# Causal mask moved from a TensorE product into a fused VectorE add-and-minimum, in a small language-model layer on one core

## The chip, the cores and the metric

The kernel runs on one core of one Trainium2 chip. Such a core has a matrix engine (TensorE, PE in the rows, with its weight loads apart as PEld), a vector engine (VectorE, DVE), a scalar engine (ScalarE, ACT), GpSimd (POOL) and SyncE (SP, which issues transfers). Each takes its own instructions in order, and they meet by semaphores. TensorE writes its results into PSUM, a memory of eight banks of 512 float32 per partition; VectorE and ScalarE read them there. The metric is the device time of one execution in microseconds (us), lower is better.

## The reference

2 x 1024 tokens run through an embedding (hot rows directly, cold rows through a projection), one attention block and one mixture of experts with 16 experts, two of them per token. The change lies in the attention, 16 heads of 32 columns, of which this is the core:

```python
att = jnp.einsum('bhqd,bhkd->bhqk', q, k) / math.sqrt(HEAD_DIM)
causal = jnp.triu(jnp.ones((s, s), dtype=bool), k=1)
att = jnp.where(causal[None, None, :, :], jnp.float32(-1000000000.0), att)
att = jax.nn.softmax(att, axis=-1)
out = jnp.einsum('bhqk,bhkd->bhqd', att, v)
```

## The kernel before, in words

The program runs embedding and first normalisation (to about 135 us of the profile), attention (to about 632 us), then output projection, router, shared expert and routed experts.

Attention is cut into 8 units: 4 groups of 4 heads, times 2 sequences. Unit 0 and unit 7 are written out, units 1 to 6 are three turns of a hardware loop. A unit has 32 steps; step n treats query block i = n // 4 (128 queries) and head h = n % 4, against the (i + 1) x 128 keys up to the diagonal. So a score row has 128 columns at i = 0 and 1024 at i = 7.

What one step asks of the engines:

- **scores** (TensorE, L499): one or two products give the negated scores in one of two pairs of PSUM banks (step n uses pair n % 2); the query side was scaled by -1/sqrt(32) before. They wait until the exponentials of step n - 2 have freed that pair. Then **L501**, a 128 x 128 bf16 product of an identity with `mask_bf`, adds 1e9 above the diagonal to the block of columns that lies on the diagonal. Its end tells VectorE that the scores are ready.
- **row_max** (VectorE, L635): a minimum over the (negated) score row, `nmax`.
- **exp** (ScalarE, L594): exp(nmax - x) for the whole row into `probs`, with the row's sum read out by a second instruction. Its end frees the PSUM pair and releases what comes next.
- **turn** (TensorE, L512): the i + 1 blocks of `probs` are turned into PSUM; ScalarE (L579) and, for a second bank where i is 4 or more, VectorE (L581) copy them to `probsT`.
- **heads** (TensorE, L525 and L528), once per four steps: product with the values, and the turned reciprocals of the row sums. ScalarE copies the latter (L601, `z_rows`) and VectorE multiplies (L649, `attnT`).
- **fill_piece** (TensorE, L478 and L483): a piece of the projection of the next unit, in every unit but the last; its results are copied by ScalarE and VectorE (L453, L457, L464, L466).

In program order TensorE does, in step n: scores(n + 1), turn(n - 1), a fill piece, and in every fourth step (n % 4 = 2) heads of the block before. VectorE does row_max(n), a projection copy, the copies of n - 2, and at n % 4 = 0 the reciprocals (L641, L643) and at n % 4 = 3 the multiplication L649, which waits for `z_rows`. ScalarE does the copies of n - 2, exp(n), and at n % 4 = 3 the `z_rows` copy.

`mask_bf` is made by GpSimd at the very start of the program: a memset of 128 x 128 (L1370) as one of several, and a select (L1397) that is the last of the nine constants for which VectorE, ScalarE and TensorE wait before their first work.

Of the kernel before, what the change touches and what calls it, by code (L numbers as in the profile page):

```python
# [62 lines left out]
def build(nc, a, out):  # L63
    ctx = ExitStack()
    with ctx:
# [10 lines left out]
        ones_bf = sb("ones_bf", [P, P], BF16)  # L76
        mask_bf = sb("mask_bf", [P, P], BF16)
        iota_bf = sb("iota_bf", [P, 256], BF16)
# [161 lines left out]
        s_dve2 = sem("dve_router_step")  # L240
        s_passed = sem("pool_waits_passed")
        s_moec = sem("router_constants_ready")
        s_wo = sem("output_weights_loaded")
# [244 lines left out]
        def att_pe(pe):  # L488
            def scores(u, b, n):
                i, h = n // GH, n % GH  # L490

                pe.wait_ge(s_E, HEAD + u * STEPS + n - 1)
                dst = bank(2 * (n % 2), 2)
                qs = q_stack[b][:, h, i * P:(i + 1) * P]
                for c0 in range(0, (i + 1) * P, 512):

                    c1 = min(max((i + 1) * P, c0 + 256), c0 + 512)
                    own = c0 <= i * P < c1
                    mm = pe.matmul(dst[:, c0:c1], qs, k_stack[b][:, h, c0:c1], start=True, stop=not own)  # L499
                    if own:  # L500
                        mm = pe.matmul(dst[:, i * P:(i + 1) * P], ident_bf[:, :], mask_bf[:, :], start=False,  # L501
                                       stop=True)
                mm.then_inc(s_S, 1)
# [124 lines left out]
        def att_dve(dve):  # L628
            def row_max(u, n):
                i = n // GH  # L630
                dve.wait_ge(s_S, HEAD + u * STEPS + n + 1)

                dve.wait_ge(s_E, HEAD + u * STEPS + n - 3)

                dve.tensor_reduce(nmax[:, n % 4:n % 4 + 1], bank(2 * (n % 2), 2)[:, 0:(i + 1) * P], AX.X,  # L635
                                  ALU.min).then_inc(s_M, 1)

# [727 lines left out]
        def _(pool):  # L1365
            for s in (s_lo, s_hi):
                pool.sem_inc(s, HEAD)
            pool.memset(xn[:, 0, :], 0.0).then_inc(s_zeros, 1)
            for m, v in ((ident, 0.0), (ident_bf, 0.0), (tri_bf, 1.0), (mask_bf, 0.0)):
                pool.memset(m[:, :], v).then_inc(s_pool, 1)  # L1370
# [19 lines left out]
            for m in (ident, ident_bf):  # L1390
# [5 lines left out]

            pool.affine_select(out=mask_bf[:, :], in_=mask_bf[:, :], compare_op=ALU.is_ge, fill=1e9, base=0,  # L1397
                               pattern=[[-1, P]], channel_multiplier=1).then_inc(s_const, 1)
# [290 lines left out]
```

## Time and profile before

| | us |
|---|---|
| time before, median of 3 runs | 1115.49 (1114.98 to 1116.05) |
| the profiled execution, its own time | 1113.7 |
| its span, first to last instruction | 1111.8 |
| TensorE busy, share of the span | 1005.3, 90% |
| VectorE busy | 551.8, 50% |
| ScalarE busy | 499.1, 45% |

Busy time is a union of the instructions' records. A matmul's record is longer than the time for which it holds TensorE, since matmuls are pipelined, so two starts in a row tell more of what a matmul costs than its length. "Idle before" with an arrow names what ended the idle time of that engine; "issue" is a wait for nothing that the profile shows.

### The profile page before, as it was taken

The page shows a single profiled execution, that of the slowest core. Times are in us where ns is not written, and L with a number is a line of the kernel's source. Part 1 is how long each engine was busy: PE and PEld are TensorE (multiplying, and loading weights), DVE is VectorE, ACT ScalarE, POOL GpSimd, SP SyncE. Part 2 cuts the span into 40 slices and gives each one's busy share as a digit, 9 for nine tenths or more (in the row PEclk, how much of TensorE's full clock was granted, in tenths as well). Part 3 has the DMA queues.
Part 4 walks back from the last instruction along what each step waited for, and adds up shares of the span by engine and source line. Part 5 has one row for each costly group of instructions (what it writes and reads, how often), then busy time and mean ns, then how long its engine had stood idle before and what let it go on. Part 6 is the DMA issues. An engine that isn't in the chain of part 4 may idle for free.

```text
span 1111.8 us, 22306 instructions
## 1 busy us (share of the span) xinstructions
PE 1005.3 (90%) x6879; PEld 643.5 (58%) x6880; DVE 551.8 (50%) x1422; ACT 499.1 (45%) x1195; POOL 298.5 (27%) x319
## 2 busy tenths in 40 slices
PE   6767699999989999899998899899998999899994
PEld 3323458576765857567585687778643444344442
DVE  7985347465645756365666677678511111111110
ACT  7512277676747777576768622211122222122221
POOL 1087220111102010020202036342223443344442
PEclk9889899999989999899999999999999999999998
DMA  5032733240513324041335111611288447944443
GB/s 200 29 86 83 180 77 81 67 112 6 135 45 77 78 57 98 32 110 45 78 78 192 41 75 58 244 69 48 78 253 237 89 89 198 290 87 85 94 85 47
DMA packets 44573, 114.37 MB, mean 103 GB/s; under 512 B 9332, under 2 KB 11380, under 8 KB 42162
## 3 DMA queue, kind: packets, MB, share of 16 engines
q1 hardware_dynamic: 32146, 87.14, 26.7%
q0 software_dynamic: 12320, 25.90, 11.9%
q8 instruction: 55, 0.90, 0.3%
q14 instruction: 52, 0.43, 0.1%
HBM read 53.03 MB, written 25.17 MB: 70 GB/s over the span
## 4 chain that ended last, share of the span: by engine, by line
PE 67%; DMA 9%; DVE 8%; issue 8%; POOL 4%; ACT 2%; POOLq 0%; ACTq 0%; DVEq 0%
PE psum L512 10%; PE psum L1241 10%; PE psum L478 7%; DMA out<-y_sb,slot_out 7%; PE psum L525 7%; PE psum L499 7%; PE psum L483 5%; PE psum L1320 5%; PE psum L1185 4%; PE psum L1169 3%; PE psum L1262 2%; PE psum L528 1%; PE psum L501 1%; PE psum L1284 1%; DMA x_rows<-xn_scratch,slot_tok 1%
## 5 line engine op out<-in xcount | busy, mean ns | idle before, releaser
L635 DVE TENSOR_REDUCE nmax<-psum 128x1 f32<-128x128 f32 (+7 forms) x256 | 192.3, 754 | 79.4 <-PE psum L501 72.2
L594 ACT ACTIVATE probs<-psum,nmax 128x128 f32<-128x128 f32 (+7 forms) x256 | 190.7, 745 | 51.0 <-DVE nmax L635 45.7
L1241 PE MATMUL psum<-attnT,x_T 128*128 x376 | 180.9, 604 | 4.2 <-issue 2.4
L512 PE MATMUL psum<-ident,probs 128*128 128x128 f32 x1152 | 176.1, 279 | 3.9 <-DVE probsT L581 1.5
L499 PE MATMUL psum<-k_stack,q_stack 128*128 128x512 f32 (+2 forms) x384 | 158.2, 466 | 22.5 <-issue 14.3
L579 ACT COPY probsT<-psum 128x512 f32<-128x512 f32 (+3 forms) x256 | 129.1, 504 | 57.4 <-PE psum L512 45.6
L1142 DVE COPY x_T<-psum 128x512 f32<-128x512 f32 x47 | 32.5, 692 | 240.5 <-PE psum L1284 240.5
L478 PE MATMUL psum<-xnT,w_unit 128*128 128x512 f32 x256 | 132.6, 608 | 0.2 <-ACT full L453 0.2
L512 PEld LDWEIGHTS psum<-ident,probs 128*128 128x128 f32 x1152 | 125.6, 143 | 9.1 <-DVE probsT L581 3.8
L425 POOL CAST part_hi<-full 128x512 fp32r<-128x512 f32 x32 | 19.6, 612 | 376.6 <-ACT full L453 268.7
L842 POOL DMA_INDIRECT out<-y_sb,slot_out x47 | 74.5, 1586 | 166.5 <-DMA out<-y_sb,slot_out 74.3
L1241 PEld LDWEIGHTS psum<-attnT,x_T 128*128 128x128 f32 x376 | 66.0, 191 | 79.9 <-issue 79.5
L499 PEld LDWEIGHTS psum<-k_stack,q_stack 128*128 128x128 f32 x384 | 69.4, 203 | 65.2 <-ACT probs L594 32.3
L1320 PE MATMUL psum<-w_dn,gated_T 128*128 x188 | 89.8, 600 | 1.0 <-ACT gated_T L894 1.0
L525 PE MATMUL psum<-probsT,v_unit 128*32 128x128 f32 x2304 | 78.5, 281 | 0.8 <-ACT probsT L579 0.8
L925 ACT ACTIVATE y_sb<-psum,slot_w 128x512 f32<-128x512 f32 x47 | 32.3, 687 | 103.6 <-PE psum L1320 61.5
L525 PEld LDWEIGHTS psum<-probsT,v_unit 128*32 128x32 f32 x2304 | 60.7, 112 | 28.6 <-ACT probsT L579 19.4
L649 DVE TENSOR_TENSOR attnT<-psum,z_rows 128x128 f32 (+1 forms) x64 | 18.7, 292 | 117.1 <-ACT z_rows L601 117.1
L483 PE MATMUL psum<-w_unit,xnT 128*128 128x128 f32 x512 | 66.7, 275 | 0.3 <-DVE full L457 0.3
L581 DVE COPY probsT<-psum 128x128 f32<-128x128 f32 (+3 forms) x128 | 61.8, 483 | 2.7 <-PE psum L512 2.5
L483 PEld LDWEIGHTS psum<-w_unit,xnT 128*128 128x128 f32 x512 | 61.7, 192 | 0.5 <-issue 0.5
L501 PE MATMUL psum<-mask_bf,ident_bf 128*128 128x128 bf16 x256 | 59.9, 234 | 0.0
(220 smaller groups left out, 1440.4 us busy)
## 6 DMA issues: line engine op xcount, KB each, us to landing
attnT<-in_wgu SPq DMA_DIRECT2D x16, 1024.0 KB, 5.2
q_stack<-part_hi SPq DMA_DIRECT2D x64, 128.0 KB, 2.4
q_stack<-part_lo SPq DMA_DIRECT2D x64, 128.0 KB, 2.4
k_stack<-part_hi SPq DMA_DIRECT2D x64, 128.0 KB, 2.4
k_stack<-part_lo SPq DMA_DIRECT2D x64, 128.0 KB, 2.6
w_dn<-in_wd SPq DMA_DIRECT2D x16, 512.0 KB, 6.1
out<-acc SPq DMA_DIRECT2D x17, 256.0 KB, 2.0
hot_all<-xn SPq DMA_DIRECT2D x4, 1024.0 KB, 8.5
```

Source lines behind the costliest of these rows:

```text
L478: mm = pe.matmul(bank(7), w_unit[:, k, side * P:(side + 1) * P], xnT[:, k, t0:t0 + 512], start=(k == 0), stop=(k == KC - 1), skip_group_ch ...
L483: mm = pe.matmul(bank(7)[:, k * P:(k + 1) * P], xnT[:, c, t0:t0 + P], w_unit[:, c, 2 * P:3 * P], start=(c == 0), stop=(c == KC - 1))
L499: mm = pe.matmul(dst[:, c0:c1], qs, k_stack[b][:, h, c0:c1], start=True, stop=not own)
L501: mm = pe.matmul(dst[:, i * P:(i + 1) * P], ident_bf[:, :], mask_bf[:, :], start=False, stop=True)
L512: mm = pe.transpose(bank(4 + m % 2)[:, (j - 4 * k) * P:(j - 4 * k + 1) * P], probs[n % PSLOTS][:, j * P:(j + 1) * P], ident[:, :])
L525: pe.matmul(bank(6)[32 * h:32 * h + 32, 0:P], v_unit[b][:, j, 32 * h:32 * h + 32], probsT[i % 2][:, h, j * P:(j + 1) * P], start=(j == 0), ...
L579: eng.copy(dst, src).then_inc(s_Ca, 1)
L594: act.activation(probs[n % PSLOTS][:, 0:(i + 1) * P], bank(2 * (n % 2), 2)[:, 0:(i + 1) * P], ACT.Exp, bias=nmax[:, n % 4:n % 4 + 1], scal ...
L635: dve.tensor_reduce(nmax[:, n % 4:n % 4 + 1], bank(2 * (n % 2), 2)[:, 0:(i + 1) * P], AX.X, ALU.min).then_inc(s_M, 1)
L842: pool.indirect_dma_start(out=out, out_offset=bass.IndirectOffsetOnAxis(ap=slot_out[:, j:j + 1], axis=0), in_=y_sb[:, j % 2, :], in_offset ...
L1241: mm = pe.matmul(bank(2 + p), lhs(k), rhs(k), start=(k == 0), stop=(k == KC - 1), skip_group_check=True)
L1320: mm = pe.matmul(bank(6 + p), gated_T[:, p, k * P:(k + 1) * P], w_dn[:, bass.ds(half, 1), k, :].rearrange("p o n -> p (o n)"), start=(k == 0),
```

## The change

`mask_bf` (128 x 128) becomes `mask_row` (128 x 1024, bf16): zeros, with the triangle of 1e9 in its last 128 columns. The product L501 is gone; the last scores product itself signals the end. VectorE's minimum becomes one fused instruction: it reads the score row from PSUM and the last (i + 1) x 128 columns of `mask_row` from SBUF, adds them, writes the sum back over the score row in PSUM, and keeps the minimum, which a second short instruction writes to `nmax`. Between its waits and the fused instruction stands an increment of a semaphore for which nobody waits (`s_dpassed`), so the waits are passed ahead of the instruction and not by it.

```diff
-        mask_bf = sb("mask_bf", [P, P], BF16)
+        mask_row = sb("mask_row", [P, QT * P], BF16)
...
-                    own = c0 <= i * P < c1
-                    mm = pe.matmul(dst[:, c0:c1], qs, k_stack[b][:, h, c0:c1], start=True, stop=not own)
-                    if own:
-                        mm = pe.matmul(dst[:, i * P:(i + 1) * P], ident_bf[:, :], mask_bf[:, :], start=False,
-                                       stop=True)
+                    mm = pe.matmul(dst[:, c0:c1], qs, k_stack[b][:, h, c0:c1], start=True, stop=True)
                 mm.then_inc(s_S, 1)
...
                 dve.wait_ge(s_E, HEAD + u * STEPS + n - 3)
 
-                dve.tensor_reduce(nmax[:, n % 4:n % 4 + 1], bank(2 * (n % 2), 2)[:, 0:(i + 1) * P], AX.X,
-                                  ALU.min).then_inc(s_M, 1)
+                dve.sem_inc(s_dpassed, 1)
+                row = bank(2 * (n % 2), 2)[:, 0:(i + 1) * P]
+                dve.tensor_tensor_reduce(out=row, in0=row, in1=mask_row[:, (QT - 1 - i) * P:QT * P], scale=1.0,
+                                         scalar=3.0e38, op0=ALU.add, op1=ALU.min,
+                                         accum_out=nmax[:, n % 4:n % 4 + 1]).then_inc(s_M, 1)
...
-            for m, v in ((ident, 0.0), (ident_bf, 0.0), (tri_bf, 1.0), (mask_bf, 0.0)):
+            for m, v in ((ident, 0.0), (ident_bf, 0.0), (tri_bf, 1.0), (mask_row, 0.0)):
                 pool.memset(m[:, :], v).then_inc(s_pool, 1)
...
-            pool.affine_select(out=mask_bf[:, :], in_=mask_bf[:, :], compare_op=ALU.is_ge, fill=1e9, base=0,
+            own = mask_row[:, (QT - 1) * P:QT * P]
+            pool.affine_select(out=own, in_=own, compare_op=ALU.is_ge, fill=1e9, base=0,
                                pattern=[[-1, P]], channel_multiplier=1).then_inc(s_const, 1)
```

What stands in a row on TensorE at the first two steps of block i = 2 in unit 0, before (scores, mask, turn, a projection piece):

```order
L499 MATMUL psum<-k_stack,q_stack 128x384 [waits probs_ready]
L501 MATMUL psum<-mask_bf,ident_bf 128x128
L512 MATMUL psum<-ident,probs 128x128 [waits probsT_copied_by_act,probs_ready]
L512 MATMUL psum<-ident,probs 128x128
L478 MATMUL psum<-xnT,w_unit 128x512 [waits projection_copied_by_act,unit_weights_loaded]
L499 MATMUL psum<-k_stack,q_stack 128x384 [waits probs_ready]
L501 MATMUL psum<-mask_bf,ident_bf 128x128
L512 MATMUL psum<-ident,probs 128x128 [waits probsT_copied_by_act,probs_ready]
```

and after:

```order
L499 MATMUL psum<-k_stack,q_stack 128x384 [waits probs_ready]
L509 MATMUL psum<-ident,probs 128x128 [waits probsT_copied_by_act,probs_ready]
L509 MATMUL psum<-ident,probs 128x128
L479 MATMUL psum<-xnT,w_unit 128x512 [waits projection_copied_by_act,unit_weights_loaded]
L499 MATMUL psum<-k_stack,q_stack 128x384 [waits probs_ready]
L509 MATMUL psum<-ident,probs 128x128 [waits probsT_copied_by_act,probs_ready]
```

One product per step is gone; nothing else moved. VectorE at block i = 2 of unit 0, from the multiplication that ends block i = 0 (L649, which waits for `z_rows`) over the four row minima of the block, before:

```order
L649 TENSOR_TENSOR attnT<-psum,z_rows 128x128 [waits z_rows_ready]
L635 TENSOR_REDUCE nmax<-psum 128x1 [waits probs_ready,scores_ready]
L641 RECIPROCAL z_rec<-z_sum 128x4 [waits heads_summed,probs_ready]
L643 COPY z_inv<-z_rec 128x128 [waits z_reciprocal_ready]
L635 TENSOR_REDUCE nmax<-psum 128x1 [waits probs_ready,scores_ready] x3
L649 TENSOR_TENSOR attnT<-psum,z_rows 128x128 [waits z_rows_ready]
```

and after:

```order
L649 TENSOR_TENSOR attnT<-psum,z_rows 128x128 [waits z_rows_ready]
L634 ISA psum,nmax<-psum,mask_row 128x384 [waits scores_ready,probs_ready]
L634 ISA nmax 128x1
L641 RECIPROCAL z_rec<-z_sum 128x4 [waits heads_summed,probs_ready]
L643 COPY z_inv<-z_rec 128x128 [waits z_reciprocal_ready]
L634 ISA psum,nmax<-psum,mask_row 128x384 [waits scores_ready,probs_ready]
L634 ISA nmax 128x1
L634 ISA psum,nmax<-psum,mask_row 128x384 [waits scores_ready,probs_ready]
L634 ISA nmax 128x1
L634 ISA psum,nmax<-psum,mask_row 128x384 [waits scores_ready,probs_ready]
L634 ISA nmax 128x1
L649 TENSOR_TENSOR attnT<-psum,z_rows 128x128 [waits z_rows_ready]
```

Each row minimum has become two instructions in the same place, behind the same neighbours; the order around them is unchanged.

## Rows read from the trace of the kernel before

**Rows 1.** The page: the chain that ended last, share of the span by engine.
```profile
PE 67%; DMA 9%; DVE 8%; issue 8%; POOL 4%; ACT 2%; POOLq 0%; ACTq 0%; DVEq 0%
```

**Rows 2.** Busy time by stretch: stretch, length, then each engine's, TensorE's granted clock, DMA.
```profile
196.20:257.70 61.50, 60.95 (x616) 43.23 (x616) 36.85 (x76) 44.16 (x109) 7.54 (x8) 1.00 0.32 73
```

**Rows 3.** Timeline in block i = 7 of unit 1: start us, length us, engine, line, operation.
```profile
250.27 0.23 PE L501 MATMUL psum<-mask_bf,ident_bf 128*128 128x128 bf16 x1
...
250.34 1.04 PE L512 MATMUL psum<-ident,probs 128*128 128x128 f32 x8
250.54 1.23 DVE L635 TENSOR_REDUCE nmax<-psum 128x1 f32<-128x1024 f32 x1 [0.52 <-PE psum L501]
...
252.57 0.23 PE L501 MATMUL psum<-mask_bf,ident_bf 128*128 128x128 bf16 x1
```

**Rows 4.** Timeline at block i = 2 of unit 1.
```profile
206.18 0.42 PE L499 MATMUL psum<-k_stack,q_stack 128*128 128x384 f32 x1
...
206.72 0.28 ACT L601 COPY z_rows<-psum 128x128 f32<-128x128 f32 x1
...
207.15 0.29 DVE L649 TENSOR_TENSOR attnT<-psum,z_rows 128x128 f32 x1 [1.10 <-ACT z_rows L601]
...
207.36 0.55 DVE L635 TENSOR_REDUCE nmax<-psum 128x1 f32<-128x384 f32 x1
...
207.94 0.58 ACT L594 ACTIVATE probs<-psum,nmax 128x384 f32<-128x384 f32 x1 [0.63 <-DVE nmax L635]
...
208.42 0.19 ACT L594 ACTIVATION_READ_ACCUMULATOR probs<-psum,nmax 128x1 f32 x1
...
208.66 0.19 PEld L499 LDWEIGHTS psum<-k_stack,q_stack 128*128 128x128 f32 x1 [0.40 <-ACT probs L594]
```

**Rows 5.** Waits of TensorE's weight loads in the attention, 135 to 636 us: total, times, longest.
```profile
PEld psum L499 <- ACT probs L594: 32.3, 57, 1.4
```

**Rows 6.** The same in unit 1, 196.2 to 257.7 us.
```profile
PEld psum L499 <- ACT probs L594: 3.1, 6, 0.9
```

**Rows 7.** The same in unit 7, 578 to 636 us.
```profile
PEld psum L499 <- ACT probs L594: 8.9, 15, 1.2
```

**Rows 8.** Waits of VectorE, 135 to 636 us.
```profile
DVE nmax L635 <- PE psum L501: 72.2, 94, 9.2
```

**Rows 9.** VectorE's groups by form: out<-in xcount, busy, mean ns, idle before.
```profile
L635 DVE TENSOR_REDUCE nmax<-psum 128x1 f32<-128x1024 f32 x32 | 39.1, 1223 | 7.9 <-PE psum L501 7.1 <-issue 0.2
...
L635 DVE TENSOR_REDUCE nmax<-psum 128x1 f32<-128x256 f32 x32 | 13.5, 423 | 15.2 <-PE psum L501 15.2
L1520 DVE SCALAR_TENSOR_TENSOR prod<-iota_bf,tok_lo,psum 128x256 f32<-128x256 bf16 x32 | 13.5, 478 | 1.7 <-PE psum L1602 1.7
...
L457 DVE COPY full<-psum 128x512 f32<-128x512 f32 x16 | 11.1, 692 | 11.0 <-PE psum L478 8.5 <-POOL part_lo L427 2.4
...
L1553 DVE TENSOR_SCALAR xn<-hot_all,mv,rstd 128x512 f32<-128x512 f32 x16 | 9.4, 586 | 6.4 <-POOL rstd L687 6.4
```

**Rows 10.** Timeline of VectorE in the embedding stage.
```profile
53.37 0.48 DVE L1520 SCALAR_TENSOR_TENSOR prod<-iota_bf,tok_lo,psum 128x256 f32<-128x256 bf16 x1
53.77 0.08 DVE L1520 DVE_READ_ACCUMULATOR prod<-iota_bf,tok_lo,psum 128x1 f32 x1
```

**Rows 11.** Timeline at the end of `z_rows` in the loop (unit 1).
```profile
256.54 0.27 ACT L601 COPY z_rows<-psum 128x128 f32<-128x128 f32 x1 [1.10 <-PE psum L528]
256.95 0.29 DVE L649 TENSOR_TENSOR attnT<-psum,z_rows 128x128 f32 x1 [1.04 <-ACT z_rows L601]
```

**Rows 12.** The same pair in unit 0, which is written out.
```profile
158.23 0.27 ACT L601 COPY z_rows<-psum 128x128 f32<-128x128 f32 x1 [0.65 <-PE psum L528]
...
158.53 0.29 DVE L649 TENSOR_TENSOR attnT<-psum,z_rows 128x128 f32<-128x128 f32 x1 [1.96 <-ACT z_rows L601]
```

**Rows 13.** Timeline of the program's start.
```profile
0.93 0.52 POOL L1368 MEMSET xn<- 128x512 f32 x1 [0.45 <-POOLq L1679]
...
1.39 0.21 POOL L1370 MEMSET ident<- 128x128 f32 x1
...
1.82 0.21 POOL L1370 MEMSET mask_bf<- 128x128 bf16 x1
1.96 0.22 POOL L1371 MEMSET ones_bf<- 128x128 bf16 x1
...
5.36 0.20 DVE L1467 CAST hot_f<-hot_ids 125x64 f32<-125x64 int32 x1 [5.36 <-POOL mask_bf L1397]
```

More of the change, by code:

```diff
@@ L241, in build @@
         s_passed = sem("pool_waits_passed")
+        s_dpassed = sem("dve_waits_passed")
         s_moec = sem("router_constants_ready")
```

## The prediction

> **What bounds the kernel now.** I read the page's chain of work first: two thirds of what ended last is TensorE [rows 1]. The change touches only the attention and the program's start, so the next view is the busy time of one attention unit: in 61.5 us TensorE's records cover 60.95, ScalarE's 44, VectorE's 37, at the full granted clock [rows 2]. That looks like a stage bound by TensorE alone, in which every product taken away is won. It is only half true, since a matmul's record outlasts its hold on the engine and hides short stalls. The weight loads show them: over the attention the load for a score product waited 57 times, 32.3 us in all, for ScalarE's exponentials [rows 5]; in unit 1 six times [rows 6], in unit 7, which has no projection to fill in, fifteen times [rows 7]. There a loop of dependences sets the pace: scores, row minimum, exponentials, and then the scores two steps later, which need the same PSUM banks. One turn of it can be followed in block i = 2: scores start at 206.18; VectorE is held until 207.15 by its multiplication, which waited for `z_rows`; the minimum runs from 207.36 to 207.91, the exponentials start at 207.94, their sum is read by 208.61, and at 208.66 the next user of those banks starts, 0.40 late [rows 4]. So the stage has two kinds of steps: those that TensorE paces, which gain by the removed product, and those in the loop, which pay for whatever VectorE's part gets longer.
>
> **The change part by part.** All sums are against the profiled execution, 1113.7 us. The median of the runs is 1115.49, 1.8 above it, and I add this difference at the end.
>
> *The product L501 goes.* From its start to that of the next matmul pass 250.34 - 250.27 = 0.07 us [rows 3]; its record of 0.23 is mostly latency. 256 of them are 17.9 us, the most that the removal can give.
>
> *How much of that reaches the end.* A scores product that waits for the exponentials of two steps before makes two steps last as long as the loop, whatever TensorE saves in them. The 57 waits are 6 in each of units 0 to 6 (42) and 15 in unit 7 [rows 5 to 7]. Some stand side by side, and such a pair covers three steps, not four, and is one turn of the loop and not two. In unit 1's timeline I count 5 turns over 12 of the 32 steps, in unit 7 10 turns over 25 steps. Together 7 x 5 + 10 = 45 turns over 7 x 12 + 25 = 109 steps. The other 256 - 109 = 147 steps gain 0.07 each: -10.3 us. In each of the 57 - 45 = 12 pairs one step between the two starts is still paced by TensorE: -0.8.
>
> *The minimum becomes a fused operation.* No row shows this instruction. The nearest is a fused instruction of the embedding stage that also reads bf16 from SBUF and float32 from PSUM, 256 columns, and keeps a result that a second instruction reads out: 478 ns against 423 for the minimum of 256 columns [rows 9]. The read-out begins 0.40 after its start and ends 0.48 after it (53.37, then 53.77 + 0.08) [rows 10]. So `nmax` is there 0.06 later than by the old instruction (0.48 against 0.42). I take this as fixed cost, at every width. The bound below is zero, as both instructions read each column of the row once; above, writing to PSUM is not in any row of VectorE. A PSUM source makes a 512-column instruction 692 ns against 586 for one that reads SBUF [rows 9], so a PSUM destination may cost up to 0.11 more. I take none of it in the forecast, as I see no sign for either end, and keep it as a rival.
>
> The Trainium skill ("Perfetto Trace Analysis", Optimizing Scalar/DVE Operations) gives VectorE a fixed data-access overhead of about 60 ns on SBUF and 125 ns on PSUM per instruction; it speaks against this change, since a destination that was in SBUF is now in PSUM. By it the sum would come out 45 x 0.065 = 2.9 us higher. No row here can show it.
>
> *The waits stand apart.* Before, the minimum carried its waits; now they are passed first, then a semaphore is raised, then the instruction is sent. The same pair shows both ways: where the multiplication carries its wait it starts 158.53 - (158.23 + 0.27) = 0.03 after `z_rows` [rows 12], where the wait stands ahead of it in the loop 256.95 - (256.54 + 0.27) = 0.14 [rows 11]. So 0.11 more from release to start. Bounds: 0, where VectorE was busy anyway and its sequencer ran ahead, and about 0.15, as there are two waits and an increment. Behind the waiting instruction stand VectorE's copies of `probsT` and the reciprocals for heads, which wait no longer than the minimum itself.
>
> *A turn of the loop* thus grows by 0.06 + 0.11 = 0.17, and is 0.07 shorter where the minimum was waiting for the mask product itself. VectorE did so in 94 of 256 steps [rows 8]; where it came from L649, as in the turn above, the product was long done. Half of the turns, rounded up: 0.17 - 0.04 = 0.13. 45 x 0.13 = +5.9 us.
>
> *The memset grows* from 128 to 1024 columns. On GpSimd 512 columns held the engine 1.39 - 0.93 = 0.46, 128 columns 1.96 - 1.82 = 0.14 [rows 13]: 0.32 for 384 columns, so 896 more cost 0.75. It has no cover: VectorE's first instruction waits for the last of these constants (the row at 5.36) [rows 13], and the whole program follows from there. +0.75 us.
>
> *The sum*: -10.3 - 0.8 + 5.9 + 0.75 = -4.4 us: 1109.3 for the profiled execution, 1111.1 against the median.
>
> **The rivals.**
>
> *A. The waits cost nothing.* VectorE's sequencer runs ahead and the increment hides. Then a turn grows by 0.06 - 0.04 = 0.02: 0.9 - 11.1 + 0.75 = -9.4, 1106.1. For it speaks that VectorE is busy little more than half of the stage, against it that it is then idle and waiting when the scores come, so the longer way from release to start is in the open.
>
> *B. Writing into PSUM costs half of its upper bound.* 0.055 more per turn: 45 x 0.055 = +2.5, which leaves -1.9: 1113.6, no measurable change.
>
> *C. The loop takes over.* The fused instruction is a special one; if its start and its write together cost 0.20 more than I priced, a turn grows by 0.33: 45 x 0.33 = 14.9, and 14.9 - 11.1 + 0.75 = +4.6: 1120.1. More steps would then join the loop, since TensorE arrives earlier and the exponentials later, and each that joins loses its 0.07 as well; 1124 is my upper end. It decides at 0.10 over my price: there 45 x 0.23 + 0.75 just eats the 11.1 us. The place is L594 waiting for VectorE, and L499 for L594. For it: 57 stalls are already there, and the margin is small; against it: the fused row I have shows a moderate fixed cost.
>
> *D. Half rate.* If reading and writing the same bank halves the rate, each column costs 1.04 ns more ((1223 - 423) / 768) [rows 9]: 1.07 us at 1024 columns, while VectorE has 0.52 idle before the minimum there in a step of 2.30 (250.27 to 252.57) [rows 3]. VectorE then paces the wide blocks, 0.5 over in each of some eight steps per unit, and the five turns of the narrower ones grow by 0.13 to 0.67, 2.0 in all: 8 x (4 + 2) = 48 us, near 1160. The Trainium skill ("Vector Engine (DVE) Microarchitecture Reference", Points that are easy to get wrong) knows such halving for two sources in SBUF that aren't bf16, which is not the case here. The embedding's fused instruction, at 478 ns for 256 columns, is not at half rate either [rows 9].
>
> **How the numbers follow.** A measurement of this kernel can tell 0.2%, 2.2 us, from no change. Forecast, -7 to -2.2 us: 0.42. A: 0.08. B: 0.22, of which a quarter falls on the faster side and the rest is no change; some of the forecast's own spread lies there too. C: 0.20. D: 0.05. The remaining 0.03 is what I have not thought of. Faster by over 0.2%: 0.50; within: 0.26; slower: 0.24. The range goes from A with a little more, 1105, to the upper end of C, 1124; D stays out.
>
> **What would show it.** In the trace of the changed kernel: the matmuls L512 following a scores product about 0.07 earlier, at unchanged clock (right or wrong: the first term); the fused instruction and its read-out ending 0.06 later than the minimum of the same width (by more: B or C; at about twice the length: D); from the end of a scores product to VectorE's start 0.11 more than before (none: A); the waits of score loads for ScalarE grown from 57 times and 32.3 us to some 65 to 75 times and about 40 us (far more: C); VectorE's first instruction at about 6.1 instead of 5.36. The forecast is wrong if the unit that now takes 61.5 us [rows 2] doesn't come down by 0.5 to 1 us.

## The result, and the profile after

The kernel after takes 1106.36 us (median of 20 runs, 1104.19 to 1111.52), the kernel before beside it 1113.61. The ratio is 0.9937, 95% interval [0.9925, 0.9949]: 7.0 us faster, 5.7 to 8.4. The profiled execution has a span of 1106.0 us, 5.8 less than before.

The page, the chain that ended last by engine (before: [rows 1]):

```profile
PE 63%; issue 10%; DMA 10%; DVE 8%; POOL 4%; ACT 3%; POOLq 0%; DVEq 0%; ACTq 0%
```

TensorE's share is four points smaller, and "issue", time in which nothing that the profile shows is waited for, grew by two. Busy time in units 1 and 6 (stretch, length, then PE, PEld, DVE, ACT, POOL, granted clock, DMA):

```profile
197.60:258.50 60.90, 59.00 (x585) 43.73 (x585) 38.84 (x108) 43.39 (x107) 7.52 (x8) 1.00 0.32 73
513.00:573.30 60.30, 58.91 (x584) 43.70 (x584) 38.67 (x108) 43.35 (x107) 7.54 (x8) 1.00 0.32 71
```

Unit 1 came down by 0.6, from 61.5 [rows 2]. Unit 6 came down by 1.0; before it was:

```profile
517.40:578.70 61.30, 60.70 (x618) 43.15 (x616) 36.89 (x76) 44.00 (x108) 7.53 (x8) 1.00 0.31 70
```

TensorE has 31 and 34 matmuls less and 1.8 to 2.0 us less busy time, VectorE 1.8 to 2.0 more. The clock didn't change.

VectorE's groups by form (mean ns of one behind the bar; before: [rows 9]). Each fused instruction has a read-out behind it:

```profile
L634 DVE CUSTOM_DVE_ANT_0 psum<-psum,mask_row 128x1024 f32<-128x1024 f32 x32 | 39.4, 1233 | 5.4 <-PE psum L499 4.8
L634 DVE DVE_READ_ACCUMULATOR2_ANT nmax<- 128x1 f32 x256 | 36.2, 141 | 0.1
...
L634 DVE CUSTOM_DVE_ANT_0 psum<-psum,mask_row 128x256 f32<-128x256 f32 x32 | 13.8, 432 | 12.9 <-PE psum L499 7.7 <-ACT probs L591 4.9
```

1233 ns at 1024 columns and 432 at 256, where the minimum took 1223 and 423 [rows 9]: the same rate per column, with add, mask and write to PSUM included. Rival D is out.

The turn of the loop that the prediction follows in block i = 2 of unit 1 (before: [rows 4]):

```profile
208.30 0.29 DVE L649 TENSOR_TENSOR attnT<-psum,z_rows 128x128 f32 x1 [0.92 <-ACT z_rows L598]
208.59 0.57 DVE L634 CUSTOM_DVE_ANT_0 psum<-psum,mask_row 128x384 f32<-128x384 f32 x1
...
209.07 0.14 DVE L634 DVE_READ_ACCUMULATOR2_ANT nmax<- 128x1 f32 x1
...
209.24 0.58 ACT L591 ACTIVATE probs<-psum,nmax 128x384 f32<-128x384 f32 x1 [0.83 <-DVE nmax L634]
...
209.97 0.19 PEld L499 LDWEIGHTS psum<-k_stack,q_stack 128*128 128x128 f32 x1 [0.79 <-ACT probs L591]
```

From L649's start to the row operation it is 208.59 - 208.30 = 0.29, before 0.21. From there to the exponentials it is 0.65, before 0.58. The weight load for the scores then comes 0.79 late instead of 0.40. Where VectorE stands idle when the scores come, the way from the product's end to its start grew more. In block i = 7:

```profile
250.55 0.70 PE L499 MATMUL psum<-k_stack,q_stack 128*128 128x512 f32 x2
...
251.09 1.04 PE L509 MATMUL psum<-ident,probs 128*128 128x128 f32 x8
251.47 1.23 DVE L634 CUSTOM_DVE_ANT_0 psum<-psum,mask_row 128x1024 f32<-128x1024 f32 x1 [0.35 <-PE psum L499]
```

The scores end at 251.25 and VectorE starts at 251.47, 0.22 later. Before it was 250.54 - (250.27 + 0.23) = 0.04 [rows 3].

Waits over the attention, 135 to 636 us (total, times, longest; before: [rows 5] and [rows 8]):

```profile
PEld psum L499 <- ACT probs L591: 51.3, 91, 1.4
```

```profile
DVE psum L634 <- PE psum L499: 52.5, 86, 9.2
```

TensorE's loads wait 91 times for the exponentials instead of 57. That is more than the 65 to 75 of the prediction.

The start of the program (before: [rows 13]): the memset holds GpSimd 2.71 - 1.82 = 0.89 instead of 0.14, and VectorE starts 0.75 later, as predicted.

```profile
1.82 0.96 POOL L1370 MEMSET mask_row<- 128x1024 bf16 x1
2.71 0.21 POOL L1371 MEMSET ones_bf<- 128x128 bf16 x1
...
6.11 0.20 DVE L1468 CAST hot_f<-hot_ids 125x64 f32<-125x64 int32 x1 [6.11 <-POOL mask_row L1398]
```

**Where the 8 us are.** A finer view than the units: the starts of ScalarE's exponentials in the timeline give the length of every block of four steps. The attention, first to last exponential, took 491.9 us before and 483.9 after. I sort the blocks in four sums. "At the turns" are the last and the first block around the two jumps back of the hardware loop, 4 of 64 blocks.

| us | unit 0 | units 1 to 6, away from the turns | at the turns | unit 7 | sum |
|---|---|---|---|---|---|
| before | 60.4 | 334.8 | 47.8 | 48.8 | 491.9 |
| after | 59.3 | 331.2 | 44.6 | 48.7 | 483.9 |
| difference | -1.1 | -3.6 | -3.2 | -0.1 | -8.0 |
| the prediction's working (units 1 to 6 whole) | -0.8 | -4.9 | none | +0.5 | -5.2 |

The -4.9 was worked out for all 48 blocks of units 1 to 6; the 44 away from the turns have -4.5 of it by their number. With the memset's 0.75 the measured sum is -7.2, close to the -7.0 of the times. The 44 blocks away from the turns repeat within 0.03 us from unit to unit, odd and even units taken apart and but for the first of unit 1 and the last of unit 6, so this sum can be trusted to a few tenths. The whole is less steady. Embedding and norm ended, and the first exponential started, between 135.7 and 139.2 in the profiles of this study, with no order by kernel (135.7 before, 138.2 after). What follows the attention took 483.6 to 487.8. So a single span isn't read here to better than some 4 us, and the two spans differ by less (5.8) than the attentions do.

Two questions are left. Are the prediction's terms right, or only their sum? And what gained 3.2 us at the turns?

### The profile page after: what moved, and what is told of

Read it like the earlier page. It is cut to its first block, busy times and chain, and to the rows that moved or that the text cites. A ratio compares the mean times of both kernels' runs of the same rounds, so it can differ in the third digit from the quotient of the medians.

```text
span 1106.0 us, 22074 instructions
## 1 busy us (share of the span) xinstructions
PE 991.0 (90%) x6623; PEld 646.6 (58%) x6624; DVE 565.8 (51%) x1678; ACT 494.3 (45%) x1195; POOL 299.2 (27%) x319
## 4 chain that ended last, share of the span: by engine, by line
PE 63%; issue 10%; DMA 10%; DVE 8%; POOL 4%; ACT 3%; POOLq 0%; DVEq 0%; ACTq 0%
PE psum L509 10%; PE psum L1241 9%; DMA out<-y_sb,slot_out 9%; PE psum L479 7%; PE psum L499 7%; PE psum L522 6%; PE psum L484 5%; PE psum L1320 5%; PE psum L1185 4%; PE psum L1169 3%; PE psum L1262 2%; PE psum L525 1%; PE psum L1284 1%; DMA x_rows<-xn_scratch,slot_tok 1%; POOL hot_all L1408 1%
## 5 line engine op out<-in xcount | busy, mean ns | idle before, releaser
L634 DVE CUSTOM_DVE_ANT_0 psum<-psum,mask_row 128x128 f32<-128x128 f32 (+7 forms) x256 | 195.4, 766 | 74.3 <-PE psum L499 52.5
L499 PE MATMUL psum<-k_stack,q_stack 128*128 128x512 f32 (+2 forms) x384 | 155.6, 460 | 28.7 <-issue 15.7
L509 PEld LDWEIGHTS psum<-ident,probs 128*128 128x128 f32 x1152 | 138.9, 143 | 35.4 <-issue 15.4
L499 PEld LDWEIGHTS psum<-k_stack,q_stack 128*128 128x128 f32 x384 | 69.6, 204 | 78.5 <-ACT probs L591 51.3
L649 DVE TENSOR_TENSOR attnT<-psum,z_rows 128x128 f32 (+1 forms) x64 | 18.7, 292 | 106.7 <-ACT z_rows L598 106.7
L888 ACT ACTIVATE silu_g<-psum 128x256 f32<-128x256 f32 x63 | 24.1, 383 | 78.7 <-PE psum L1241 63.4
```

The lines of the kernel that those rows point to most:

```text
L509: mm = pe.transpose(bank(4 + m % 2)[:, (j - 4 * k) * P:(j - 4 * k + 1) * P], probs[n % PSLOTS][:, j * P:(j + 1) * P], ident[:, :])
L634: dve.tensor_tensor_reduce(out=row, in0=row, in1=mask_row[:, (QT - 1 - i) * P:QT * P], scale=1.0, scalar=3.0e38, op0=ALU.add, op1=ALU.min, ...
```

## Experiments: the two sides of the change apart

All ratios are to the kernel before on the same chip. Block sums and waits come from one profile of each kernel.

**The products' side alone.** The mask is left out, and nothing takes its place:

```diff
-                    own = c0 <= i * P < c1
-                    mm = pe.matmul(dst[:, c0:c1], qs, k_stack[b][:, h, c0:c1], start=True, stop=not own)
-                    if own:
-                        mm = pe.matmul(dst[:, i * P:(i + 1) * P], ident_bf[:, :], mask_bf[:, :], start=False,
-                                       stop=True)
+                    mm = pe.matmul(dst[:, c0:c1], qs, k_stack[b][:, h, c0:c1], start=True, stop=True)
```

> The kernel before without the mask product L501, and with nothing in its place: the causal mask is left out of the computation. This measures what TensorE's side of the change gives. Theory T, the sum of the prediction: the 147 steps outside the loop of dependences gain 0.07 us each (-10.3), the 12 pairs 0.07 (-0.8), and the 45 turns of the loop get shorter by 0.04 (-1.8): -12.9 us, ratio 0.988. Rival R2: the product costs more than the distance of two starts, because the load of its identity is not hidden and TensorE's pair of waits moves too: -16 us or more, ratio 0.985 or less. If it is under -9 us, ratio over 0.992, the gain of the change came from somewhere else.

Measured: 0.9878 [0.9854, 0.9901], -13.6 us. Away from the turns units 1 to 6 take 325.8, which is 9.0 less than before. The products' term of units 1 to 6 was 6 x 1.47 = 8.8, some 8.1 for these 44 of their 48 blocks, so it holds to about a tenth. How it is spread differs: a step became 0.089 shorter at i = 7 (2525 to 2436 ns), 0.079 at i = 6 and 0.077 at i = 2, but only 0.020 at i = 4 and 0.006 at i = 0. More score loads now wait for the exponentials:

```profile
PEld psum L498 <- ACT probs L590: 48.6, 85, 4.1
```

Much of the growth from 57 to 91 waits is here already, with VectorE's instruction untouched: TensorE comes earlier to the same exponentials. The longest of them, 4.1 us, is a turn of the hardware loop. The time alone lies between theory T (-12.9) and R2 (-16 or more), and its interval, 11.0 to 16.3, doesn't keep them fully apart.

**VectorE's side alone.** The fused operation and the long memset as in the kernel after, and the mask product kept as well, so the mask is added twice:

```diff
-                dve.tensor_reduce(nmax[:, n % 4:n % 4 + 1], bank(2 * (n % 2), 2)[:, 0:(i + 1) * P], AX.X,
-                                  ALU.min).then_inc(s_M, 1)
+                dve.sem_inc(s_dpassed, 1)
+                row = bank(2 * (n % 2), 2)[:, 0:(i + 1) * P]
+                dve.tensor_tensor_reduce(out=row, in0=row, in1=mask_row[:, (QT - 1 - i) * P:QT * P], ...
```

> The changed kernel with the mask product put back on TensorE, so that the mask is added twice: this measures VectorE's side alone (fused operation, waits apart, longer memset). Theory T: 45 turns of the loop grow by 0.06 + 0.11, +7.7 us, and the memset costs 0.75: +8.4 us, ratio 1.0075. Rival R1: the waits apart cost nothing, because VectorE is held by other work when most score rows come: 45 x 0.06 + 0.75 = +3.5 us, ratio 1.003.

Measured: 1.0031 [1.0015, 1.0047], +3.5 us, the rival's number. But away from the turns the six units take 339.3, 4.5 more than before, and at the turns 44.5, 3.3 less, as in the kernel after. So a cost of the size that the theory gives (30 turns at 0.17, 5.1) is there where no turn is near, and a gain at the turns hides part of it. Its score loads wait 84 times, 43.4 us in all, so this side alone raises the count as much as the missing product does.

The two sides alone, -13.6 and +3.5, make -10.1, and together they gave -7.0. The intervals of the times cover this difference; in the blocks, which are finer, -9.0 + 4.5 = -4.5 stands against -3.6, so together they gain about 1 us less than apart.

**The memset alone**, in the kernel before (the mask product reads the last 128 columns):

```diff
-            for m, v in ((ident, 0.0), (ident_bf, 0.0), (tri_bf, 1.0), (mask_bf, 0.0)):
+            for m, v in ((ident, 0.0), (ident_bf, 0.0), (tri_bf, 1.0), (mask_row, 0.0)):
```

> The kernel before with the long row of zeros: memset of 1024 columns at the start, the mask product reads its last 128. Nothing else. Theory T: VectorE starts 0.75 us later and nothing recovers it: +0.75 us, ratio 1.0007. Rival: in the changed kernel's trace the first score minimum came 2.5 us later than before; if all of that belongs to the memset (a later start that meets the gathers badly, or addresses that moved by 1792 bytes), +2.5 us, ratio 1.0022.

Measured: 1.0018 [1.0002, 1.0034], +0.2 to +3.8 us, which holds the 0.75, and the 2.5 of the rival too. VectorE's first instruction is at 6.12. Its blocks are the best check of those before: 334.9 away from the turns (334.8 before), 48.6 at the turns (47.8).

**The waits apart**, with the plain minimum:

```diff
                 dve.wait_ge(s_E, HEAD + u * STEPS + n - 3)
+                dve.sem_inc(s_dpassed, 1)
                 dve.tensor_reduce(nmax[:, n % 4:n % 4 + 1], bank(2 * (n % 2), 2)[:, 0:(i + 1) * P], AX.X,
```

> The kernel before with one semaphore increment between the waits and the row minimum, so that the waits stand apart as in the changed kernel; minimum and mask product stay. Theory T: 0.11 us in each of 45 turns of the loop: +5.0 us, ratio 1.0045; in the trace the minimum starts 0.11 later after the end of the product. Rival R1: +1 us or less, ratio 1.001.

Measured: 1.0019 [1.0003, 1.0035], +2.1 us. The price itself is there, and larger than the 0.11 of the prediction. Where VectorE stands idle, as here in block i = 7, the product ends at 252.79 and VectorE starts 0.18 later instead of 0.04:

```profile
252.56 0.23 PE L502 MATMUL psum<-mask_bf,ident_bf 128*128 128x128 bf16 x1
252.97 1.23 DVE L637 TENSOR_REDUCE nmax<-psum 128x1 f32<-128x1024 f32 x1 [0.51 <-PE psum L502]
```

Over all steps with an idle VectorE the median goes from 0.038 to 0.179, +0.14. Yet the six units away from the turns lose only 1.1 us (335.9), where the prediction's 30 turns at 0.11 make 3.3. The place where it was charged wrongly is in the same trace: behind L649, where VectorE comes late itself and both semaphores have long been raised, the minimum starts 0.25 after it instead of 0.21 (L649 is L651 here, L635 is L637).

```profile
209.32 0.29 DVE L651 TENSOR_TENSOR attnT<-psum,z_rows 128x128 f32 x1 [0.96 <-ACT z_rows L602]
209.57 0.56 DVE L637 TENSOR_REDUCE nmax<-psum 128x1 f32<-128x384 f32 x1
```

So 0.14 is paid where VectorE was waiting, which it did 109 times in the attention; a loss of 1.1 us over 44 blocks says that most of it is taken up behind it. Where VectorE comes late itself it is 0.04.

**The same without the mask products**, since the loop of dependences could be tighter there:

> The kernel before without the causal mask (the mask products are left out, and nothing takes their place), and with VectorE's increment between the two waits and the plain minimum. What tells is the difference from the run without the mask alone (0.9878; unit 6, which no turn of the loop touches, 59.7 us) to this one. Theory T (a turn grows by the price of waiting apart, 0.14 us by the run with the mask products, on some 45 turns): +6 us, ratio 0.993, unit 6 at about 60.5. Rival V (as with the mask products, where it gave +2.1 us and +0.2 in unit 6, VectorE has slack for 0.14, and it is the fused operation's later result that bites): +2 us, ratio 0.9895, unit 6 at 59.9.

Measured: 0.9933 [0.9912, 0.9953], against 0.9878 without the increment. The times speak for T (+6 us), the blocks for V: unit 6 takes 59.8 instead of 59.7,

```profile
507.80:567.60 59.80, 58.74 (x584) 43.81 (x584) 37.24 (x76) 43.59 (x108) 7.52 (x8) 1.00 0.31 72
```

and away from the turns it is 327.1 against 325.8, +1.3. The six runs of this kernel spread from 1099.7 to 1109.1, and the profiled one is the fastest. What made the others longer isn't in any trace that I have, so this stays open. For the mechanism I go by the blocks, which repeat.

## Experiments: the turns of the hardware loop

At a jump back of the loop (two of them, near 318 and 448 us) TensorE, VectorE and ScalarE stand still for 3.1 to 4.4 us in the kernels before and after. This is VectorE before, at the first one:

```profile
322.56 0.29 DVE L635 TENSOR_REDUCE nmax<-psum 128x1 f32<-128x128 f32 x1 [3.95 <-PE psum L501]
322.78 0.69 DVE L581 COPY probsT<-psum 128x512 f32<-128x512 f32 x1
323.39 0.17 DVE L641 RECIPROCAL z_rec<-z_sum 128x4 f32<-128x4 f32 x1
325.58 0.23 DVE L643 COPY z_inv<-z_rec 128x128 f32<-128x128 f32 x1 [2.02 <-issue]
```

There are two stalls, the jump itself and 2.02 more for nothing that the profile names, in front of L643. That second one stands at the same place at both turns (2.02 and 1.27), in the kernel without the mask (1.81 and 1.22) and in the one with the long memset (1.49 and 1.43); with the increment it stands one instruction earlier (1.45 and 1.42, and 1.17 and 1.30 without the mask product). In the kernel after it isn't there, nor in the one that has the fused operation and the mask product:

```profile
322.77 0.30 DVE L634 CUSTOM_DVE_ANT_0 psum<-psum,mask_row 128x128 f32<-128x128 f32 x1 [4.43 <-issue]
...
323.05 0.69 DVE L578 COPY probsT<-psum 128x512 f32<-128x512 f32 x1
323.66 0.17 DVE L641 RECIPROCAL z_rec<-z_sum 128x4 f32<-128x4 f32 x1
323.86 0.23 DVE L643 COPY z_inv<-z_rec 128x128 f32<-128x128 f32 x1
```

The four blocks at the turns take 45.7 to 49.0 us in the six looped kernels with the plain minimum, and 43.1 to 44.6 in the three with the fused operation.

The trace also lists the transfers that bring instructions. In the kernel before, three of them, of 8 and 16 KB, start between 319.5 and 319.9, inside the stall, and three more between 322.6 and 323.0, at its end. A seventh starts at 326.17, 0.6 after the second stall, and at the other turn at 456.36, again 0.6 after it. Every looped kernel with the second stall has this one at both turns, 0.6 to 0.9 after it. The kernel after and the one with the fused operation and the mask product have neither the stall nor this transfer. So both stalls go with the loading of instructions. That the engines waited for it is my reading, as no row names it.

My guess was that the place of the loop's code in VectorE's stream decides whether there is a second stall. The code can be shifted without any other change, by increments ahead of unit 0, where VectorE is idle:

```diff
+            for _ in range(16):
+                dve.sem_inc(s_dpad, 1)
             unit(0, 0, 0, None, True)
```

> The kernel before with 16 idle semaphore increments on VectorE ahead of unit 0, where it waits some 7 us anyway: all that follows stands 16 instructions further on in its stream, and nothing else is changed. Theory S (part of the change's gain is a second stall of VectorE, 1.3 to 2.1 us at its tenth instruction after each of the two turns of the hardware loop, which depends on where the loop's head stands in the stream): the stall is gone or elsewhere, the first blocks after the turns take about 2150 to 2250 ns a step instead of 2838 and 2189, and the time falls by 2 to 3 us, ratio about 0.9978. Rival M (the stall goes with the plain minimum and its waits, wherever they stand): the stall stays, ratio 1.000.

Measured: 1.0007 [0.9991, 1.0023]. In the trace the second stall is gone from both turns:

```profile
323.20 0.69 DVE L582 COPY probsT<-psum 128x512 f32<-128x512 f32 x1
323.81 0.17 DVE L642 RECIPROCAL z_rec<-z_sum 128x4 f32<-128x4 f32 x1
324.01 0.23 DVE L644 COPY z_inv<-z_rec 128x128 f32<-128x128 f32 x1
324.20 0.29 DVE L636 TENSOR_REDUCE nmax<-psum 128x1 f32<-128x128 f32 x1
```

and the blocks at the turns take 45.7 instead of 47.8, -2.1. But away from them the six units take 335.8, 1.0 more, nearly all of it in one block that did not exist as an odd one before: i = 5 of the odd units takes 2308 to 2314 ns a step instead of 2222. So the shift took a stall away at one place and added a cost at another. In this profile the attention is still 1.9 us shorter (489.9), but the times don't show it: their interval is -1.0 to +2.6 us. The seventh transfer of instructions is gone from both turns as well. The place of the code matters, which refutes rival M for the stall (it should have stayed wherever the minimum stands). That it is worth 2 to 3 us of time, as I expected, isn't borne out.

The opposite, the kernel after shifted by 32:

> The kernel after with 32 idle semaphore increments on VectorE ahead of unit 0. The loop's head then stands at row 630 of VectorE's records instead of 598, as far ahead of a multiple of 64 as in the kernel before (566). Theory S: the second stall appears at about the tenth instruction after both turns, and 2 to 3 of the change's 7 us are lost, ratio to the kernel before about 0.996. Rival M: no second stall, ratio 0.9937 as the kernel after.

Measured: 0.9948 [0.9929, 0.9966]. The second stall did not come back, and the blocks at the turns take 43.1. So the rule of 64 in my expectation is wrong. The shift was seen again away from the turns: in the odd units a step takes 2116 ns instead of some 2206 at i = 4 and 2372 instead of 2438 at i = 7, but 1577 instead of 1521 at i = 2 and 2344 instead of 2256 at i = 6; their sum is 331.0, as before the shift (331.2). I have no rule for the places, only that they move with the code. The attention in this profile is 3.2 us shorter than in the kernel after (480.7), and the times are no better (0.9948 against 0.9937): a gain of that size in one profile's attention need not be one of the kernel.

**Without any turn.** The loop over units 1 to 6 is written out on all five engines, in the kernel before and in the kernel after:

```diff
-            with dve.Fori(0, GROUPS - 1) as g:
+            for g in range(GROUPS - 1):
```

> The kernel before with the hardware loop over units 1 to 6 written out on all five engines: no turns. After the two turns the first blocks of four steps take 2838 and 2189 ns a step, where the first block of other units takes about 1662: 4 x 1.18 + 4 x 0.53 = 6.8 us. Theory S: the time falls by about 6.8 us, ratio 0.994. Rival (what stalls there is the first pass over new code, which written-out units pay too): ratio 1.000 or above.

> The kernel after with the same loop written out. Its first blocks after the turns take 2158 and 2258 ns a step against about 1677: 4 x 0.48 + 4 x 0.58 = 4.2 us to gain, ratio to the kernel before about 0.9899. What tells theories apart is the difference from the written-out kernel before: theory S expects the sum of the prediction, -4.4 us, without what the turns gave; if the turns have no part in the change's gain it is -7 us as with the loop.

> The kernel before without the causal mask and with the loop written out: the split of the change's gain where no turn disturbs it. Written out, a unit takes 61.1 us before and 59.8 after. Theory T expects 59.6 or less here (the products' 11.1 us over 8 units are 1.4, and by the run with the loop 1.6) and so leaves 0.2 to 0.8 us a unit for VectorE's side; rival: the products give 1.4 a unit and VectorE's side costs next to nothing, a unit at 59.7. Ratio to the kernel before about 0.976 by T, 0.981 by the rival.

> The kernel before without the causal mask, with the increment between VectorE's two waits and the loop written out: the step between the written-out kernel without the mask (a unit takes 59.4 us) and the written-out kernel after (59.8), whose only further difference is the fused operation in place of the minimum. Theory T, 0.14 us for waiting apart and 0.07 for the later result acting alike: two thirds of the 0.4, a unit at 59.65, ratio about 0.977. Rival V (there is slack for the first 0.14, and the later result bites): a unit at 59.5, ratio 0.9755.

Measured: before 1098.29 us, 0.9873 [0.9848, 0.9897]; after 1092.6 us, 0.9818 [0.9794, 0.9842]; without the mask 0.9753 [0.9730, 0.9776]; without the mask and with the waits apart 0.9761 [0.9736, 0.9787]. Writing out gives more than the 6.8 and 4.2 us that I had read from the first blocks behind the turns: some 16 and 14 us by the medians. In the profiles the attention is 17.5 and 17.3 us shorter, of which the four blocks at the turns give 14.1 and 11.9, and the 44 away from them 1.6 and 4.7. The rival, that the first pass over new code costs as much, is out.

Between the two written-out kernels lie 5.7 us, by the spread of their six runs each known to some 2. That is between the 4.4 of theory S and the 7 with the turns' part, and rules out neither. In the profiles the attention gains 7.9 us written out and 8.0 in the loop. So the change is worth about as much without any turn as with two. Unit 6 of the written-out kernel before, and of the one after:

```profile
502.70:563.80 61.10, 60.70 (x618) 43.20 (x616) 36.96 (x76) 44.22 (x108) 7.54 (x8) 1.00 0.31 70
```

```profile
494.40:554.20 59.80, 58.95 (x585) 43.85 (x584) 38.74 (x108) 43.72 (x109) 7.53 (x8) 1.00 0.31 72
```

And without the mask, with the waits together and apart:

```profile
493.40:552.80 59.40, 58.63 (x584) 43.91 (x584) 36.82 (x76) 43.90 (x109) 7.53 (x8) 1.00 0.32 72
```

```profile
491.50:550.90 59.40, 58.62 (x585) 43.88 (x584) 37.02 (x76) 43.72 (x108) 7.52 (x8) 1.00 0.32 72
```

Here odd and even units hardly differ (single blocks do, as i = 3 of unit 4, 0.2 to 0.3 us longer in each of these four), and the blocks at the former turns take 33.7 (before) and 32.7 us (after) like the same blocks of other units. The split over the same 44 blocks, written out beside looped; the prediction's column is for all 48 blocks of the six units:

| us, units 1 to 6 away from the turns | predicted | looped | written out |
|---|---|---|---|
| products gone | -8.8 | 334.8 to 325.8: -9.0 | 333.1 to 323.8: -9.3 |
| waits apart | +3.3 | +1.1; without the mask 325.8 to 327.1: +1.3 | 323.8 to 324.1: +0.2 |
| fused operation for the minimum | +0.6 | with the product 335.9 to 339.3: +3.4; without 327.1 to 331.2: +4.1 | 324.1 to 326.4: +2.4 |
| sum | -4.9 | 334.8 to 331.2: -3.6 | 333.1 to 326.4: -6.7 |

Written out, the four blocks at the former turns are whole blocks like the others, so there all 48 can be set against the prediction: products -10.0 (-8.8 predicted), waits 0.0 (+3.3), fused operation +2.3 (+0.6), together -7.7 (-4.9).

The times of the whole program give the same for the products, 13.4 us written out and 13.6 in the loop. For VectorE's side with the memset they give 7.2 (0.9753 to 0.9818) and 6.6 (0.9878 to 0.9937), known to some 3 or 4. Theory T's 12.9 and 8.4 are near both.

Rival V holds for the waits: written out they cost almost nothing, though VectorE's start after an idle time is 0.14 later there too (median 0.038 to 0.178). Behind L649 nothing is lost: where its scores have long ended (up to i = 3) the row operation starts 0.21 after it in all of these kernels, the fused one too. In the loop, the fused operation starts 0.29 after it. That difference may be part of why VectorE's side costs 2.6 us written out and 5.4 in the loop. Writing the loop out also puts fixed numbers for the waits that the loop counts from its own counter; the runs don't separate the two.

**A version that beats both kernels.** The kernel after written out, and of the wide mask row only the last 128 columns zeroed ahead of the constants, the rest by a second memset behind them, for which VectorE waits before the attention:

```diff
-            for m, v in ((ident, 0.0), (ident_bf, 0.0), (tri_bf, 1.0), (mask_row, 0.0)):
+            for m, v in ((ident, 0.0), (ident_bf, 0.0), (tri_bf, 1.0), (mask_row[:, (QT - 1) * P:QT * P], 0.0)):
...
+            pool.memset(mask_row[:, 0:(QT - 1) * P], 0.0).then_inc(s_maskz, 1)
```

> The kernel after with the loop over units 1 to 6 written out, and of the wide mask row only the last 128 columns zeroed ahead of the constants, the other 896 by a second memset behind them. Both theories expect VectorE's first instruction back near 5.4 us, 0.75 us earlier than in the kernel after, and units of 59.8 us: ratio 0.981 (0.9818 written out without the late zeros), and unit 0 starts 0.75 us earlier, as far as the stage ahead of it repeats.

Measured: 1090.1 us, 0.9792 [0.9775, 0.9809], the fastest of the kernels that apply the mask. VectorE starts at 5.36 again, but its first instruction takes 0.74 instead of 0.20, while the second memset runs beside it:

```profile
5.21 0.83 POOL L1402 MEMSET mask_row<- 128x896 bf16 x1
5.36 0.74 DVE L1470 CAST hot_f<-hot_ids 125x64 f32<-125x64 int32 x1 [5.36 <-POOL mask_row L1399]
...
6.13 0.20 DVE L1471 TENSOR_SCALAR hot_wrap<-hot_f 125x64 f32<-125x64 f32 x1
```

The same second instruction starts at 6.34 in the written-out kernel after: 0.2 of the 0.75 came back, the rest was lost again. The remaining difference between the two medians, 2.5 us, is inside the intervals. The Trainium skill ("SBUF — State Buffer", SBUF: two separate sides) says that a GpSimd instruction and a VectorE instruction in a mode that uses two ports share a pair of ports to SBUF as an exclusive lock, held for a whole instruction; by that rule the cast, if it ran in such a mode, was kept out for the memset's length. The trace agrees in that the cast ends 0.06 after the memset's record; in which mode it ran no run shows.

## Why the prediction was right, and where it wasn't

The time lies in the range, the sign is right, and the forecast of 1111.1 is 4.7 us too high. Of these, 1.9 are its starting point, a median of 3 runs (1115.49) where 20 runs give 1113.61; the rest is the gain, 4.4 expected and about 7 measured. That 1106.36 falls on rival A's 1106.1 is luck: A had only one of its two prices right. Step by step:

- **Products: right to about an eighth.** Written out, -10.0 against -8.8 over units 1 to 6. The step behind it was too simple: steps gain between 0.006 (i = 0) and 0.089 (i = 7) rather than 0.07 or nothing, and the number of turns of the dependence loop isn't fixed. It grew from 57 score waits to 85 by the removal alone.
- **Waits apart: price too small, term too large.** 0.14 instead of 0.11 from release to start, but +1.1 us instead of +3.3. The step that failed is the one that charged the price to all 45 turns. In the very turn that I had followed, VectorE came late from L649, with both semaphores passed; there the price is 0.04 in the loop and none written out. Rival A's size (nothing) was nearly right for this term. Its mechanism, that the increment hides, holds behind L649 alone: where VectorE waits the 0.14 is in the open, and is taken up later.
- **The fused operation: mis-sized.** Priced at 0.06 on the result, less 0.04 for the product that VectorE no longer waits for. Measured from the start of the row operation to the exponentials it is 0.07 (0.65 for 0.58 at i = 2), and its start is 0.04 later besides, both where VectorE was idle (0.178 to 0.218) and behind L649 in the loop (0.25 to 0.29). The 0.07 is the same at 384 to 1024 columns, in the medians over all steps where ScalarE stands waiting (0.582 to 0.659 at 384, 1.391 to 1.460 at 1024). Together 0.11, on every step that VectorE paces: +3.4 and +4.1 us instead of +0.6. Rival B's half price for writing to PSUM, 0.055, is about what is missing from 0.06 to 0.11. Whether it is the destination that costs it, I can't say, since no run had the fused operation write elsewhere. The Trainium skill's 0.065 more for an instruction on PSUM ("Perfetto Trace Analysis", Optimizing Scalar/DVE Operations) isn't refuted by this either.
- **That the sum came near is in part luck.** The waits were priced too high and the fused operation too low. In the loop these errors nearly cancelled (-3.6 in the 44 blocks where -4.5 was worked out); written out they didn't quite (-7.7 for -4.9). Rival C, which decides at 0.10 over the price of a turn, didn't come about: the fused operation lies 0.05 over its price, and the waits, 0.03 over theirs where VectorE stands idle, under it where it is late.
- **Memset: right**, 5.36 to 6.11.
- **Missing: the turns of the hardware loop.** -3.2 of the -8.0 us in the attention's profile. The trace of before has both stalls of VectorE at each turn, "issue" among them, and I had read past them. For the second stall the runs show that it comes and goes with where the code stands. That the whole -3.2 would come again with another layout isn't shown: shifting the kernel before took 2.1 off the same blocks and left the time unchanged. So part of the looped kernel's gain, between 0 and some 3 us, may be an accident of placement. The change doesn't depend on it: written out, with no turn, it gives 5.7 us. There it gains more away from the former turns (6.7 for 3.6), so the loop takes about as much from it there as it gives at the turns.
- **What would show it.** VectorE's first instruction and the unit's length (0.6 and 1.0 for 0.5 to 1) came as written; the length of the fused operation too. The score waits, 91 and 51.3 us for 65 to 75 and 40, should have sent me to C or B by my own list. But the missing product alone brings them to 85 and VectorE's side alone to 84, so a high count doesn't tell C or B from a gain, which the list had not allowed for. The fused operation without the increment between wait and instruction wasn't tried.

## What to carry to other kernels

A cost on one engine is charged only where that engine is the late one: for each turn of a dependence loop ask whether the engine stands waiting (then the way from release to start can count, as far as what follows has no slack) or comes late itself (then waits are already passed, and mostly the length of its own instructions counts). Removing work from the bounding engine can add waits by itself, here from 57 to 85, so such a count taken before a change is no fixed number in its sum. And a hardware loop's turns belong in the list of what is read: here writing the loop with its two turns out gave 14 to 16 us of 1114, twice what the change gave, and moving code about changed single blocks of the odd units by up to 0.4 us in every pass.

## What the runs showed of the hardware that I had not expected

- At a jump back of the hardware loop TensorE, VectorE and ScalarE stood still for 3.1 to 4.4 us, with transfers of instructions inside the stall. Written out, the same work takes 15.7 us less (1114.0 to 1098.29, the kernel before, two jumps).
- In the loop, single blocks of four steps are 0.2 to 0.4 us longer or shorter by where the code stands (i = 5 at 2222 or 2312 ns a step, i = 4 at 2116 or 2206, i = 6 at 2256 or 2344). Written out, odd and even units agree but for single blocks (i = 3 of unit 4, 1739 for 1689).
- A fused add-and-minimum with both result and row in PSUM runs at the rate of the plain minimum, 1233 and 1223 ns at 1024 columns, and its price over the minimum is about 0.11 us (0.07 on the result, 0.04 on the start). The fused instruction itself is 9 to 20 ns longer at every width.
- Beside a GpSimd memset of 0.83 us a VectorE cast of 125 x 64 took 0.74 us instead of 0.20.
